# A grouped convolution turned round: stationary weights, columns gathered by DMA through DRAM

## What is computed

```
x = x + L0_ffn(L0_cond(x, cond))
x = x + L1_ffn(L1_cond(x, cond))

L0_cond: a 32x32 mix of the channels per batch entry (weights from an MLP on cond), plus a bias
L0_ffn:  rank-16 products of 4 experts, the best 2 by a router: delta = sum(gate * B A x)
L1_cond: conv_general_dilated(x, weight[32, 8, 9], padding 4, feature_group_count=4)
         + cond @ c_weight.T + fside
L1_ffn:  x @ weight.T plus a rank-16 product of 8 experts, the best 2 by a router with a norm;
         an expert that is chosen more often than its capacity allows is dropped
```

## Time and profile before

| | us |
|---|---|
| median of 3 runs | 371.43 |
| lowest and highest run | 370.94, 371.61 |
| span of the profiled execution, first to last instruction | 368.9 |

### The profile page before, as it was taken

One profiled execution on the slowest core, in us unless ns is written; L12 is line 12 of the kernel. 1 busy time (PEld: TensorE's weight loads), 2 busy tenths in 40 slices (PEclk: granted clock), 3 DMA queues, 4 the chain that ended last, 5 costly groups with the idle time before them and its releaser, 6 DMA issues.

```text
span 368.9 us, 6652 instructions
## 1 busy us (share of the span) xinstructions
PE 334.9 (91%) x2312; PEld 304.6 (83%) x2312; DVE 266.3 (72%) x618; ACT 121.2 (33%) x266; POOL 91.1 (25%) x123
## 2 busy tenths in 40 slices
PE   4998879998999799979997999799999998988994
PEld 3697768996999699969996999799989987866662
DVE  1776999648864887488757875787579537479997
ACT  4333655214521352135214521352115311113320
POOL 5212131114111411141114111411121202126650
PEclk9999999999999999999999999999999999999999
DMA  7760133000301030003000300000000000001877
GB/s 161 172 142 9 32 135 115 0 30 0 116 0 30 0 115 1 30 1 115 3 28 0 114 0 28 0 0 0 28 0 2 2 0 3 0 0 56 304 289 264
DMA packets 18792, 21.46 MB, mean 58 GB/s; under 512 B 8356, under 2 KB 8836, under 8 KB 18768
## 3 DMA queue, kind: packets, MB, share of 16 engines
q1 hardware_dynamic: 18064, 20.92, 17.4%
q0 software_dynamic: 272, 0.21, 0.6%
q10 hardware_dynamic: 432, 0.02, 0.1%
HBM read 12.74 MB, written 8.40 MB: 57 GB/s over the span
## 4 chain that ended last, share of the span: by engine, by line
issue 40%; PE 27%; DVE 20%; POOL 9%; DMA 2%; DVEq 1%; ACT 1%; POOLq 0%
PE ps_c L1145 7%; POOL o1l L452 6%; PE ps_d L1032 6%; PE ps_g L1032 4%; PE ps_a L1001 3%; DVE xT L977 2%; DVE y_all L863 2%; DVE xp L977 2%; DMA y_all<-in_L_ffn_Wr_dram 2%; DVE o L857 1%; DVE xp L871 1%; POOL mixbd L411 1%; PE ps_d L1075 1%; DVE hb L842 1%; DVE ha L843 1%
## 5 line engine op out<-in xcount | busy, mean ns | idle before, releaser
L1145 PE MATMUL ps_c<-cw,xp 128*128 128x128 f32 x768 | 91.5, 276 | 1.6 <-DVE xp L871 1.6
L1145 PEld LDWEIGHTS ps_c<-cw,xp 128*128 128x128 f32 x768 | 88.7, 192 | 2.7 <-issue 1.8
L452 POOL TENSOR_TENSOR o1l<-o,o1h 128x512 fp32r<-128x512 f32 x32 | 41.5, 1297 | 165.4 <-ACT o1h L538 165.4
L1032 PE MATMUL ps_d<-wt_hi,o1h 128*128 128x336 f32 (+1 forms) x128 | 44.5, 348 | 0.7 <-issue 0.3
L558 ACT ACTIVATE xp<-y_all 32x512 f32 (+2 forms) x68 | 40.1, 590 | 11.4 <-DVE y_all L863 10.5
L1032 PE MATMUL ps_d<-wt_hi,o1l 128*128 128x336 f32 (+1 forms) x128 | 41.9, 327 | 0.0
L1032 PE MATMUL ps_d<-wt_lo,o1h 128*128 128x336 f32 (+1 forms) x128 | 41.7, 326 | 0.0
L857 DVE TENSOR_TENSOR o<-ps_c,bias 128x512 f32<-128x512 f32 x32 | 22.0, 689 | 25.4 <-PE ps_c L1145 25.0
L863 DVE TENSOR_TENSOR y_all<-ps_d,xs 128x512 f32<-128x512 f32 (+1 forms) x32 | 33.1, 1069 | 3.8 <-PE ps_d L1171 3.8
L1032 PE MATMUL ps_g<-wt_hi,o1l 128*128 128x336 f32 x112 | 35.5, 317 | 0.0
L1032 PE MATMUL ps_g<-wt_hi,o1h 128*128 128x336 f32 x112 | 35.5, 317 | 0.0
(11 more groups left out here) (219 smaller groups left out, 577.9 us busy)
## 6 DMA issues: line engine op xcount, KB each, us to landing
xs<-in_x_dram SPq DMA_DIRECT2D x7, 1024.0 KB, 5.4
out_dram<-xT SPq DMA_DIRECT2D x16, 256.0 KB, 2.0
out_dram<-xp SPq DMA_DIRECT2D x16, 256.0 KB, 2.2
bias<-cbias SPq DMA_DIRECT2D x8, 256.0 KB, 3.2
xs<-in_x_dram SPq DMA_DIRECT2D x2, 512.0 KB, 5.9
y_all<-in_L_ffn_weight_dram SPq DMA_DIRECT2D x1, 1024.0 KB, 10.3
y_all<-in_L_ffn_lora_B_dram SPq DMA_DIRECT2D x1, 256.0 KB, 6.6
ga<-in_L_ffn_lora_A_dram SPq DMA_DIRECT2D x8, 32.0 KB, 5.1
```

Source lines behind the costliest of these rows:

```text
L452: pool.tensor_tensor(o1l[t % 2][:, :, :], o1[t % 2][:, :, :, :].rearrange("p q b c -> p q (b c)"), o1h[t % 2][:, :, :].bitcast(fp32), ALU. ...
L1032: last = T.matmul(bank[:, 0:columns], a[t % 2][:, q, :], w[:, q, first:first + columns], start=(q == 0 and n == 0), stop=(q == Q - 1 and n ...
L1145: last = T.matmul(ps_c[:, b * P:(b + 1) * P], xp[par][:, b, t, j:j + M], cw[:, j, :, :].rearrange("p q o -> p (q o)"), start=(j == 0), sto ...
```

## The change

A convolution now has the weights stationary and the data moving, and positions are stored by their residue modulo 8. Each finished tile of x1 is written to DRAM (`write`, 256 KB) and read back by four DMAs (`gather`) into xg, for each of the four groups separately: on the 128 partitions lie the eight residues of the group's eight channels and, from a column further left or right, the residues that the border taps need. A tile's convolution is four products, one for each group, with 64 columns of weights and 256 moving columns; the outputs of the groups lie by turns on partitions 0 to 63 and 64 to 127. DVE adds the bias, which now lies per partition in `biasT`, and writes oT. Four DMAs (`hop`) move oT into oz, from even and odd partitions into halves, and PE transposes oz for its four batch entries (`o_transposed`) into the layout that the main product needs. ACT copies that twice out of PSUM, rounded and plain. The copies into xp, the bias loads and their buffers are gone.

The order on each engine is rewritten: convolutions of tiles 0 and 1 of a step are issued in the step before, and the transposes of a tile's output some products later. On ACT a middle step has gm_out, the four copies of xT, o_hi(1), ga_out(0), u_out, o_hi(2), the first exponential, hidden_out, ga_out(1), o_hi(3), the second exponential, ga_out(2), o_hi(s+1, 0) and ga_out(3). In step -1 DVE has w_lo(0), w_lo(1), x1 of four tiles, o_out(0, 0), w_lo(2), w_lo(3) and o_out(0, 1). In setup the main product's weights are permuted by four copies on ACT ahead of their transposes (two of the four transposes move ahead of the u products of step 1), the taps are loaded by four DMAs in runs of nine floats, four times as many in all as before, and lora_a by 16 DMAs instead of 8.

```diff
-    SH = 3
+    QH = 2 * Q
+    MH = H // QH
+    G = C // CG
+    GP = G // 2
+    NTAP = 20
...
-xp = [sb(f"xp{i}", [P, BT, NT, M + 2]) for i in range(2)]
-o1 = [sb(f"o1_{i}", [P, Q, BT, C]) for i in range(2)]
+xg = sb("xg", [P, 2, BT, G, MH])
+oT = sb("oT", [P, 2, GP, BT, MH])
+oz = sb("oz", [P, 2, BT, 2, MH])
+o1 = [sb(f"o1_{i}", [P, Q, P]) for i in range(2)]
...
-bias = [sb(f"bias{i}", [P, NT, BT, C]) for i in range(2)]
+biasT = sb("biasT", [P, GP, NB])
...
-cw = sb("cw", [P, SH, Q, C])
+cw = sb("cw", [P, G, Q, CG, 2])
...
-cbias = nc.dram_tensor("cbias", (NB * C,), fp32).ap()
+x1d = nc.dram_tensor("x1d", (NS * NT, 2, P, H // 2), fp32).ap()
...
+    def write(u, t):
+        wait(sp, s_x1, u * NT + t + 1)
+        sp.dma_start(x1d[bass.ds(u * NT + t, 1)].rearrange("n h p c -> p (n h) c"),
+                     y_all[:, bass.ds(u * ST + t * H, H)].rearrange("p (h c) -> p h c", h=2))\
+          .then_inc(s_x1w[t], 16)
+    def gather(u, t):
+        wait(sp, s_x1w[t], (u + 1) * 16)
+        half = [x1d[bass.ds(u * NT + t, 1), h].rearrange("n (b g c) (q m) -> (n c q) (b g) m",
+                                                         b=BT, c=CG, q=Q) for h in range(2)]
+        dst = xg[:, t % 2].rearrange("p b g m -> p (b g) m")
+        sp.dma_start(dst[C:2 * C], half[0]).then_inc(s_xg[t % 2], 16)
+        sp.dma_start(dst[2 * C:3 * C], half[1]).then_inc(s_xg[t % 2], 16)
+        sp.dma_start(dst[0:C, :, 1:MH], half[1][:, :, 0:MH - 1]).then_inc(s_xg[t % 2], 16)
+        sp.dma_start(dst[3 * C:4 * C, :, 0:MH - 1], half[0][:, :, 1:MH]).then_inc(s_xg[t % 2], 16)
+    def hop(u, t):
+        wait(sp, s_ob, u * NT + t + 1)
+        for p in range(GP):
+            for z in range(2):
+                sp.dma_start(oz[2 * C * p:2 * C * (p + 1), t % 2, :, z, :],
+                             oT[z:P:2, t % 2, p]).then_inc(s_hop[t % 2], 16)
+    sp.wait_ge(s_zero, 4)
     def step(s, par, k):
-        if has(s, 0) and has(s, 2):
-            wait(sp, s_x1, s * NT + NT)
+        if at_step(s, NS):
+            hop(s - 1, 2)
+            hop(s - 1, 3)
+            return
+        if at_step(s, 0):
+            write(s, 0)
+            write(s, 1)
+            gather(s, 0)
+            write(s, 2)
+            write(s, 3)
+            gather(s, 1)
+        else:
+            if at_step(s, 1):
+                hop(s - 1, 2)
+            for t in range(NT):
+                write(s, t)
+        if has(s, 2):
             sp.dma_start(xs[par][:, :, :],
                          x_v[bass.ds(s + 2, 1)].rearrange("s p t h -> p (s t) h")).then_inc(s_x[par], 16)
-        if has(s, 0) and has(s, 1):
-            wait(sp, s_o1, s * NT)
-            sp.dma_start(bias[1 - par][:, :, :, :].rearrange("p t b c -> p (t b c)"),
-                         cbias[bass.ds((s + 1) * (NT * P), NT * P)].partition_broadcast(P))\
-              .then_inc(s_bias[1 - par], 16)
-    steps(sp, step, -1, NS - 1)
+        if not at_step(s, 0):
+            if not at_step(s, 1):
+                hop(s - 1, 2)
+            gather(s, 0)
+            hop(s - 1, 3)
+            gather(s, 1)
+        hop(s, 0)
+        gather(s, 2)
+        hop(s, 1)
+        gather(s, 3)
+    steps(sp, step, 0, NS)
...
+    def o1_low(u, t):
+        pool.wait_ge(s_o1, u * NT + t + 1)
+        pool.wait_ge(s_o1h, u * NT + t + 1)
+        pool.tensor_tensor(o1l[t % 2][:, :, :], o1[t % 2][:, :, :], o1h[t % 2][:, :, :].bitcast(fp32),
+                           ALU.subtract).then_inc(s_o1l, 1)
...
+    def o_in(t):
+        return ps_t[:, :].rearrange("p (b q o) -> p q b o", q=Q, o=CG)
+    def o_hi(u, t):
+        act.wait_ge(s_tp, u * NT + t + 1)
+        wait(act, s_mp, u * NT + t - 1)
+        nc.scalar.activation(o1h[t % 2][:, :, :].rearrange("p q (b o) -> p q b o", o=CG), o_in(t),
+                             ACT.Copy).then_inc(s_o1h, 1)
+        nc.scalar.activation(o1[t % 2][:, :, :].rearrange("p q (b o) -> p q b o", o=CG), o_in(t),
+                             ACT.Copy).then_inc(s_o1, 1)
...
+    def o_out(u, t):
+        dve.wait_ge(s_cp, u * NT + t + 1)
+        wait(dve, s_tp, u * NT + t - 1)
+        V.tensor_tensor(oT[:, t % 2, :, :, :], ps_c[:, :].rearrange("p (g b m) -> p g b m", g=GP, b=BT),
+                        row(biasT[:, :, bass.ds(u * (NT * BT) + t * BT, BT)], 3, MH), ALU.add)\
+         .then_inc(s_ob, 1)
...
+        def x1_next(t):
             dve.wait_ge(s_dp, (s + 1) * NT + t + 1)
+            V.tensor_tensor(y_all[:, bass.ds((s + 1) * ST + t * H, H)].rearrange(mq, q=QH),
+                            ps_d[t % 2][:, :].rearrange(mq, q=QH),
+                            xs[1 - par][:, t, :].rearrange(qm, q=QH), ALU.add).then_inc(s_x1, 1)
...
         if at_step(s, 0):
             gates0(1)
+            o_out(s, 2)
             y_out(s, 0)
+            for t in range(NT):
+                x1_next(t)
+        else:
+            for t in range(NT):
+                x1_next(t)
+            o_out(s, 2)
+            norm_first(s - 1)
+            y_out(s, 0)
+            norm_last(s - 1)
+        o_out(s, 3)
         if has(s, 2):
             gates0(s + 2)
+        y_out(s, 1)
+        o_out(s + 1, 0)
+        if has(s, -1):
+            choices(s - 1)
+        y_out(s, 2)
+        o_out(s + 1, 1)
+        y_out(s, 3)
...
+    def conv(u, t):
+        pe.wait_ge(s_xg[t % 2], (nth(u, t) + 1) * 64)
+        wait(pe, s_ob, u * NT + t)
+        for g in range(G):
+            n = g // 2 * (BT * MH)
+            last = T.matmul(ps_c[2 * C * (g % 2):2 * C * (g % 2 + 1), n:n + BT * MH],
+                            cw[:, g, :, :, :].rearrange("p q o z -> p (q o z)"), xg[:, t % 2, :, g, :],
+                            start=True, stop=True)
+        last.then_inc(s_cp, 1)
+    def o_transposed(u, t):
+        pe.wait_ge(s_hop[t % 2], (nth(u, t) + 1) * 64)
+        if t == 3 and not at_step(u, 0):
+            pe.wait_ge(s_ht, u)
+        elif t == 1 and not at_step(u, 0) and has(u, 1):
+            pe.wait_ge(s_gt, u + 2)
+        elif t == 2 and at_step(u, 0):
+            pe.wait_ge(s_gt, 2)
+        elif t == 0 and at_step(u, 0):
+            pe.wait_ge(s_gt, 1)
+        else:
+            pe.wait_ge(s_o1, u * NT + t)
+        for b in range(BT):
+            last = T.transpose(ps_t[:, b * P:(b + 1) * P],
+                               oz[:, t % 2, b, :, :].rearrange("p z m -> p (z m)"), idp)
+        last.then_inc(s_tp, 1)
...
+        if at_step(s, -1):
+            gm_transposed()
+            u_products(1, (2,))
+            pe.wait_ge(s_gt, 1)
+            delta(0)
+            delta(1)
+            u_products(1, (3,))
+            delta(2)
+            delta(3)
+            mix(1)
+            w_transposed(2)
+            w_transposed(3)
             pe.wait_ge(s_cw, 1)
             pe.wait_ge(s_zero, 4)
+            pe.wait_ge(s_wlo, 1)
+            conv(0, 0)
+            conv(0, 1)
+            o_transposed(0, 0)
+            return
...
         if at_step(s, NS - 1):
+            conv(s, 2)
+            o_transposed(s, 1)
+            gates(0)
+            conv(s, 3)
             main(s, 0, (0, 1))
+            o_transposed(s, 2)
+            gates(1)
+            hidden_transposed()
+            main(s, 0, (2,))
+            o_transposed(s, 3)
+            gates(2)
             router()
             main(s, 0, (3,))
             gates(3)
             main(s, 1)
             main(s, 2, (0, 1, 2))
             return
+        ahead = has(s, 2)
+        if at_step(s, 0):
+            conv(s, 2)
+            o_transposed(s, 1)
+            pe.wait_ge(s_wlo, Q)
+            x_transposed(0)
+            x_transposed(1)
             main(s, 0)
+            x_transposed(2)
+            x_transposed(3)
+            gm_transposed()
+            u_products(s + 2)
+            pe.wait_ge(s_gt, s + 2)
+            delta(0)
+            delta(1)
+            conv(s, 3)
+            delta(2)
+            o_transposed(s, 2)
+            delta(3)
+        else:
+            gm_transposed()
+            conv(s, 2)
+            if ahead:
+                x_transposed(0)
+            pe.wait_ge(s_gt, s + 2)
+            delta(0)
+            delta(1)
+            if ahead:
+                x_transposed(1)
+            else:
+                o_transposed(s, 1)
+            delta(2)
+            if ahead:
+                x_transposed(2)
+                x_transposed(3)
+            delta(3)
+            if ahead:
+                o_transposed(s, 1)
+            main(s, 0)
+            if ahead:
+                u_products(s + 2)
+            conv(s, 3)
+            o_transposed(s, 2)
         if ahead:
             mix(s + 2)
+        main(s, 1)
+        if has(s, -1):
+            hidden_transposed()
+        conv(s + 1, 0)
+        if has(s, -1):
+            router()
+        o_transposed(s, 3)
+        main(s, 2)
+        conv(s + 1, 1)
+        o_transposed(s + 1, 0)
+        main(s, 3)
```

More of the change, by code:

```diff
@@ L610, in step @@
[L610 to L623 removed]
+                        x_transposed(s + 2)
```

553 lines of the change are left out of this document (209 added, 344 removed).

## The result

The changed kernel takes **355.04 us** (median of 4, 353.57 to 356.41) where the one before took 371.52 (median of 4 in the same session): a ratio of 0.956, interval 0.953 to 0.959. The forecast was 353.0. The profiled execution took 353.9 us, its span is 352.2.

What follows compares the result with a forecast made beforehand. PE was taken to set the pace. Start +7, steps 1 to 5 -17, step 6 -0.8 and step 7 -7.5 sum to -18.3: span 368.9 becomes 350.6, with 2.5 added 353 us; range 333 to 378.

Steps and rivals of the forecast that it cites:

- So per tile 2.68 - 1.8 - 0.4 = 0.5 us: PE's gain per convolution tile: old convolution 2.68 us, less new one 1.8 and four new transposes 0.4; 1.9 us a step.
- I take 0.225: Time in us of one 256-column product record of the new convolution; 8 records make 1.8 us a tile.
- rival (a): Convolution products on the two partition halves run together: 8 records take the time of 5, 335 us in all; chance 0.15.
- Start: +7: Stretch up to step 1: it begins near 90 us instead of 82.59, 7 us later; bounds +4 and +13.
- behind it more work stands than before: PE between main(0,0) and step 1: 29.1 us of work and 1.7 of waits, where before 25.0 us led there.
- The queue: SP's DMAs per middle step: 18 + 1.6 us of issue and 21 us of engine time, within 33.8 us.
- rival (c): SP's DMA queue binds: 3.06 ns a piece instead of 1.2, 41.8 us a step, 409 us in all; chance 0.17.
- I take 0.4: SP's issue time in us for one hop DMA of 256 pieces, so a hop of four is 1.6 us.
- I still cost them at nothing, with thin cover: New waits for writes, gathers and hops on SP and PE: costed at nothing; uncovered, a step loses 1 to 3 us.
- Rival (b): Hop or gather lands 1 to 3 us late in each step, 6 or 7 times: 360 to 372 us; chance 0.15.
- Step 7: -7.5: First convolution behind step 6 to the fourth gate product: 14.6 us instead of 22.1, with 1.9 us of waits.
- Its end, the counts and the output stage stay: From the end of step 7's gate products to the kernel's end: no change, forecast 0.

## Why the prediction was right, and where it was wrong

**What bounds the kernel: right.** PE sets the pace in the steps before and after; DVE binds the end.

**"So per tile 2.68 - 1.8 - 0.4 = 0.5 us": wrong by 0.8 us a tile, the mis-sized term.** The term "I take 0.225" is right for one record behind another (0.22 in the run on one half), but the 8 records go two at a time and take the time of four and a fraction, 1.0 us. That was rival (a), priced at 0.68 us a tile less; 0.78 was found. The argument against it, that "no row has two matmuls of different columns at once", was empty: no product in the rows of the kernel before writes one half alone, so no row could have shown it. The Trainium skill, TensorE: Matmul & The Clock Gate, What picks the tile position, which the prediction named there, has the output's start partition pick the column tile. This trace agrees: two halves give 1.94 / 1.09 = 1.8 times the speed of one. The 2.38 times that the prediction quotes stands on the same page under Measured speedup vs the span model, for three tiles of 32 columns, not two of 64. With the halves side by side the steps fell by 25.6 us and not by 17. The convolutions alone would have given 15.6 more (20 x 0.78); PE was idle for 8.2 us of the five steps (160.2 - 152.1), where 2.5 were forecast, and the transposes took 0.1 us a tile more, which together take some 7 us back.

**This term decides the sign.** With all products on one half, which is the convolution as I priced it, the kernel takes 374 us, 0.7% more than before. By my sum that kernel was to take 353. So the forecast of "faster" was right for a reason that I gave 0.15, and its own mechanism alone would have ended slower. What my sum left out shows in that run's milestones: step 1 begins at 101.7 (+19.1 for +7), five steps take 172.4 (169 forecast), the rest 99.3 (92.2): 12.1 + 3.4 + 7.1 = 22.6 us, the whole difference of its span (373.3) to 350.6.

**"Start: +7": wrong by 7.2 us.** conv(0,0) at 44.2 was forecast well (45), main(0,0) came at 61.1 for 58.5. The step that failed is "behind it more work stands than before", a sum of PE work with 1.7 us of waits, where 6.3 were found: x1 of step 1 is made behind main(0,0), so its write, gather and hop ran in the open a second time, with the 1 MB load ahead of the gather: 5.8 us of wait at 84.6. The run with x1 made earlier takes the wait away. The clock has no term in the sum. To 57 us it costs nothing that the DMAs would not (the run with work in place of the waits); in the two stretches behind, it may cost up to 3.9 us, of which 2.1 stand ahead of main(0,0). No run takes these apart from the waits.

**The queue: right on the whole.** DMA share 0.65 in the steps for the 0.62 of my sum (21 of 33.8), 58% over the span, the DMAs of a gather at 0.49 to 0.55 us in the median: rival (c) did not come. The Trainium skill, DMA: Bandwidth & Descriptors, Specifications, has transfers under 512 B fall off the line rate, with a read and a modify ahead of the write. The doubling to 35 us of engine work a step that I tried on it did not show, 0.65 of a step of 32.0 us being 21. But "I take 0.4" for a hop DMA was low: 0.62 at the median, 2.6 us for four instead of 1.6. The 256 pieces of a hop cost more than 512 of a gather, and not for their step of 2. The issue sum has two slips: 4 x (2.5 + 1.6 + 0.4) and a load of 0.4 are 18.4 us a step and not "18 + 1.6", and a step has 37 DMAs, not the 33 of rival (c). By the medians measured they take 20 us of 32.0, so neither slip decided anything.

**"I still cost them at nothing, with thin cover": half wrong.** Rival (b) came in a mild form, 1.1 to 1.3 us for tile 2's hop in three steps, more when the clock fell behind it. I had looked at tile 0's hop, behind gates0, and that one came 0.2 to 0.9 us late; the later one was tile 2's, behind DVE's four x1 additions and SP's four writes. Moving it is worth 6.6 us in the totals and 4.1 in the five steps.

**"Step 7: -7.5": right**, -8.6, of which the two cheaper convolutions give 1.6; the two waits are 1.09 and 0.73 us, 1.8 for the 1.9 forecast.

**"Its end, the counts and the output stage stay": wrong by 6.3 us.** Up to the first lora product it is 18.0 us (297.2 to 315.2) for 14.2 before (320.2 to 334.4): the choices of step 6 wait for a router's product that now stands behind a transposition and a gate product, and y_out stands behind them. The run with the router earlier took 2.3 of these 3.8 us back. From there on it is 37.0 for 34.5: the step of 8 words, costed at nothing, makes the closing additions 9% slower from start to start. My upper bound of 3 us for it was the value to take, since I had found that nothing covers it.

## What to carry to other kernels

In this kernel, products whose results stand on different halves of the partitions went side by side, each with 64 weight columns; give every pair of small products one of each half, and when pricing a form that no row has, ask whether any row could have shown the overlap before counting its absence as evidence. A transfer's chain through DRAM (write, gather, move) costs its waits once in every place where nothing else is ready, so look for the second such place, not only the first. When an engine's output is moved by DMA, put the operation that feeds it first in its engine's order and its issue first in the queue: three lines moved here gave 6.6 us of 355 between the medians.

## What the runs showed of the hardware

- Two products of 128x256 with 64 weight columns each run at once, within 0.02 us of each other, and do so even when both products of one half are issued ahead of the other half's. Alone, a half takes 0.22 us a record: 1.87 us a tile from start to start, against 1.02.
- Waits of 2.4 to 3.5 us for tile 2's hop, in the middle of full work, were followed by a stretch at 1.2 GHz (6.8 us of it in one run, with PE busy for 6.3). Shorter ones went either way: one of 2.04 us in the same place, in the run with the closing step of 4, and one of 1.54 us for tile 0's hop, in the run with the hop first, were not; one of 1.61 us, in the run with the router earlier, was.
- The issue of a DMA of 256 pieces of 256 B from one on-chip buffer to another took 0.62 us at the median, with or without a step over its partitions; one of 512 pieces from DRAM took 0.49 to 0.55 at the median and 0.34 at the least.
- An addition over 128x512 f32 with an output step of 8 words took 1.20 us and 1.09 with a step of 4; with its two inputs at a step of 64 and its output at 1 it took 1.07. From start to start these are 1.01, 0.92 and 0.98 us. With no wide step it took 0.68 (y_out of step 7).
